# Dropless mixture of experts: when expert numbers, positions and one look-ahead element are read and made

## What is computed

```
h = layernorm(x)
logits = h @ rw.T + rb                    # 896 tokens, 8 experts
vals, idx = top_k(logits, 2); gates = softmax(vals)
h1 = gelu(h @ fc1_w[e] + b1[e]); eo = h1 @ fc2_w[e] + b2[e]
x = x + sum over the two chosen experts of gates * eo
...
k = ctx @ kw + kb; v = ctx @ vw           # second cross attention: of ctx alone
out = softmax(q k / 4) v
```

## Time and profile before

| | |
|---|---|
| median of 3 runs | 2123.18 us (2117.42 to 2124.7) |
| profiled execution, its own time | 2124.0 us |
| its span | 2122.2 us |
| granted TensorE clock, mean share | 0.923 |
| busy: PE, DVE, ACT, POOL | 84%, 62%, 41%, 29% of the span |
| the mixture | from 366 to 653 us of the span |
| its tile loop | from 449.65 to 620.4 us |
| loads of each tile | 1028 KB and 1024 KB of weights (first, second layer), 128 KB of rows; 128 KB of results stored |
| DMA share in the tile loop | 0.83 (464 to 541 us), 0.89 (541 to 613 us) |

### The profile page before, as it was taken

How to read it: one execution, slowest core, us unless ns; L and a number is a source line. 1 busy time by engine, 2 the same in 40 slices (tenths; PEclk the granted TensorE clock), 3 DMA queues, 4 the chain that set the end, 5 groups by cost and what they waited for, 6 DMA issues and landing times.

```text
span 2122.2 us, 34231 instructions
## 1 busy us (share of the span) xinstructions
PE 1787.3 (84%) x10658; PEld 1245.8 (59%) x10658; DVE 1323.6 (62%) x3343; ACT 860.9 (41%) x2497; POOL 618.0 (29%) x710
## 2 busy tenths in 40 slices
PE   5959997769995878998889999696886979999888
PEld 4736664558974756555755554483443845555557
DVE  5856776101115877788667767596776866656655
ACT  3735553223223642555334444242331434544421
POOL 2325554200011233676500000040000325555433
PEclk9979999789997988899889999797998989999979
DMA  4000000368972001112100010101001000000200
GB/s 165 32 23 16 15 8 27 116 223 303 305 234 105 0 1 38 45 49 83 65 15 15 8 67 0 50 1 60 0 0 43 28 1 11 22 10 11 70 1 18
DMA packets 38632, 121.21 MB, mean 57 GB/s; under 512 B 2960, under 2 KB 26032, under 8 KB 31360
## 3 DMA queue, kind: packets, MB, share of 16 engines
q1 hardware_dynamic: 32520, 104.71, 14.5%
q10 hardware_dynamic: 4472, 11.52, 1.5%
q0 software_dynamic: 1536, 3.67, 0.6%
HBM read 102.41 MB, written 17.47 MB: 56 GB/s over the span
## 4 chain that ended last, share of the span: by engine, by line
PE 46%; issue 20%; POOL 13%; DVE 11%; ACT 4%; DMA 2%; another core or an unknown queue 1%; ACTq 1%; POOLq 0%; SPq 0%; DVEq 0%
POOL arena L1902 11%; PE ps L954 8%; PE ps L989 4%; PE ps L774 3%; PE ps L826 3%; PE ps L878 3%; PE ps L1114 3%; PE ps L896 3%; PE ps L1098 3%; PE ps L769 3%; PE ps L844 2%; PE ps L816 1%; PE ps L1033 1%; DMA arena<-rows_hbm 1%
## 5 line engine op out<-in xcount | busy, mean ns | idle before, releaser
L1902 POOL TENSOR_TENSOR arena<-arena,rinv 112x375 f32<-112x375 f32 (+1 forms) x448 | 371.2, 830 | 505.9 <-DVE rinv L1570 494.2
L844 PEld LDWEIGHTS ps<-cst,arena 112*125 112x125 f32 (+1 forms) x1408 | 187.5, 183 | 176.1 <-POOL arena L1902 91.7
L844 PE MATMUL ps<-cst,arena 112*125 112x112 f32 (+1 forms) x1408 | 245.8, 293 | 44.7 <-POOL arena L1902 44.0
L1227 ACT ACTIVATE arena<-ps,negmax 112x375 f32<-112x375 f32 (+1 forms) x384 | 190.8, 502 | 178.3 <-DVE negmax L1565 177.9
L1579 DVE COPY arena<-ps 125x336 f32<-125x336 f32 x384 | 191.1, 498 | 49.5 <-PE ps L844 47.3
L1950 POOL TENSOR_TENSOR w_split_sb<-wml,w_split_sb 128x512 fp32r<-128x512 f32 (+1 forms) x40 | 46.0, 1150 | 563.3 <-ACT w_split_sb L1276 561.4
L1565 DVE TENSOR_REDUCE negmax<-ps 112x1 f32<-112x375 f32 (+1 forms) x288 | 158.2, 549 | 79.2 <-PE ps L816 69.4
L954 PE MATMUL ps<-h_split_sb,w_split_sb 128*128 128x448 f32 x768 | 178.4, 382 | 8.3 <-DVE h_split_sb L1699 4.3
L1227 ACT ACTIVATE arena<-arena,negmax 112x112 f32<-112x112 f32 (+1 forms) x256 | 125.4, 491 | 134.4 <-DVE negmax L1554 94.5
L954 PEld LDWEIGHTS ps<-h_split_sb,w_split_sb 128*128 128x128 f32 x768 | 151.8, 199 | 24.0 <-issue 5.9
L769 PE MATMUL ps<-wat,arena 128*125 128x256 f32 (+1 forms) x608 | 151.3, 386 | 7.9 <-ACT arena L1174 7.3
(11 more groups left out here) (213 smaller groups left out, 3159.8 us busy)
## 6 DMA issues: line engine op xcount, KB each, us to landing
wml<-in_wm_L_moe SPq DMA_DIRECT2D x21, 1028.0 KB, 5.6
wml<-in_wm_L_moe SPq DMA_DIRECT2D x21, 1024.0 KB, 6.1
craw<-in_ctx SPq DMA_DIRECT2D x34, 375.0 KB
wml<-in_wm_L_m SPq DMA_DIRECT2D x3, 3072.0 KB, 13.9
values_hbm<-vz ACTq DMA_DIRECT2D x8, 750.0 KB
vz<-values_hbm SPq DMA_DIRECT2D x8, 750.0 KB
wat<-in_wa_L_ca SPq DMA_DIRECT2D x2, 2560.0 KB
wml<-in_wm_L_m SPq DMA_DIRECT2D x2, 2048.0 KB, 13.0
```

The costliest lines, as they stand in the source:

```text
L844: last = nc.tensor.transpose(ps[0:blk.kp, T_BANK + s % blk.t_banks, o:o + S], buf[:, i * blk.nk + q * blk.kp:i * blk.nk + (q + 1) * blk.kp ...
L1227: last = go(probs[0:S, s % blk.nprobs, i * nk:(i + 1) * nk], src[:, i * nk:(i + 1) * nk], ACT.Exp, scale=-1.0 if blk.mask == "input" else ...
L1902: pool.tensor_tensor(p3, p3, r3, ALU.mult).then_inc(scaled, 1)
```

## The change

SyncE reads an expert number right before the load that needs it (the loads of tile t + 2 stand behind the wait for the gelu of tile t). The first rows are loaded ahead of the first second-layer weights. VectorE counts, for each token position, the experts chosen over the batches, so two matmuls are enough; it makes the part within a position itself (`within`) and adds it to the slots. Look-ahead element 4 is made behind `tile_results(18)`. The look-ahead stores values without padding (375 KB), in a part of `vz` that the self attention doesn't use; the wait for the stores goes from the mixture's end to the first keys of that attention (ScalarE) and to GpSimd's work for the next MLP, where GpSimd zeroes that part again. In the cross attention the values are loaded to `craw`, and ScalarE spreads them into `vz` with three instructions per batch, at step 12 of the batch before.

```diff
@@ load_tiles
+                chosen = []
                 def load_w1(t):
                     o = WH * (t % 2)
+                    chosen.append(sp.value_load(expert[0:1, t:t + 1], min_val=0, max_val=E - 1))
...
-                chosen = [sp.value_load(expert[0:1, t:t + 1], min_val=0, max_val=E - 1) for t in range(NT)]
                 for t in range(2):
                     load_w1(t)
-                for t in range(2):
-                    load_w2(t)
                 sp.wait_ge(scattered, 16 * TOP * B)
                 for t in range(2):
                     load_rows(t)
+                for t in range(2):
+                    load_w2(t)
@@ load_context
                             sp.wait_ge(av_done, st["group"] + (m - 1) * 4)
+                            sp.wait_ge(values_spread, m - 1)
                         sp.dma_start(kT[:, m % 2], ...)
-                        sp.dma_start(vz[0:KP, m % 2], values_hbm[m])...
+                        sp.dma_start(craw[:, m % 2], values_hbm[m]...)...
@@ tensor, weigh
+                        if blk.ahead:
+                            pe.wait_ge(values_spread, count(0, 1, b, 1))
@@ tensor, mixture
-                mm(ps[0:S, 2, 0:B * E], upper, chosen, ...)
-                for b in range(B - 1):
...
-                       start=False, stop=b == B - 2, skip_group_check=True)
-                for b in range(B):
-                    last = mm(ps[0:S, 1, 0:E], all_ones, flags[:, b], start=b == 0, stop=b == B - 1)
-                last.then_inc(placed, 1)
-                for m in range(1, 5):
+                mm(ps[0:S, 2, 0:E], cs("upper", S, S), counts, start=True, stop=True)
+                mm(ps[0:S, 1, 0:E], cs("ones", S, S), counts, start=True, stop=True).then_inc(placed, 1)
+                for m in range(1, 4):
                     context_ahead(m)
...
                     tile_results(t)
+                    if t == NT - 3:
+                        pe.wait_ge(tile_act, 2 * (NT - 2))
+                        pe.wait_ge(tile_kept, NT)
+                        context_ahead(4)
+                        pe.wait_ge(ahead_done, 5 * NAHEAD)
@@ scalar, attention: piece
                     elif name in ("K0", "K1"):
+                        if n > 0 and not blk.cross and isinstance(m, int) and m == 0:
+                            for i in range(2):
+                                act.wait_ge(ahead_stored[i], 32 * (B // 2))
@@ scalar, attention
+                def spread_values(m):
+                    par = parity(m)
+                    act.wait_ge(kv_loaded[par], pair(m) * 32 + 32)
+                    if not isinstance(m, int) or m >= 2:
+                        act.wait_ge(av_done, count(st["group"], 4, m, -4))
+                    for q in range(KC):
+                        dst = vz[0:kp, par, q * H * 32:(q + 1) * H * 32]
...
+                        last = go(dst, craw[:, par, q]..., ACT.Copy)
+                    last.then_inc(values_spread, 1)
                 for name in blk.pieces:
                     piece(0, name)
+                if blk.ahead:
+                    act.wait_ge(zeroed, 3)
+                    spread_values(0)
                 def body(b):
                     for s in steps(b, blk, lag + 1):
+                        if blk.ahead and s == 12 and more(b):
+                            spread_values(b + 1)
@@ scalar, context_ahead
-                        for i, q in enumerate([0, 1] if c == 0 else [2]):
-                            dst = vz[0:KP, m % 2, q * H * 32:(q + 1) * H * 32]
...
+                        last = go(v_ahead[:, m % 2, 0:2 * D] if c == 0 else v_ahead[:, m % 2, 2 * D:3 * D], W[0:KP, 0:(2 - c) * D], ACT.Copy)
@@ scalar, mixture
-                for m in range(5):
+                for m in range(4):
                     context_ahead(m)
...
+                    if t == NT - 2:
+                        context_ahead(4)
                 for m in range(5, B):
                     context_ahead(m)
-                for i in range(2):
-                    act.wait_ge(ahead_stored[i], 32 * (B // 2))
@@ vector, mixture
-                v.tensor_scalar(flags, rank, float(TOP), None, ALU.is_lt).then_inc(flagged, 1)
+                link(v.tensor_scalar(flags, rank, float(TOP), None, ALU.is_lt))
+                by_expert = flags.rearrange("p b e -> p e b")
+                v.tensor_reduce(counts, by_expert, AX_X, ALU.add).then_inc(flagged, 1)
+                for b in range(B):
+                    last = v.tensor_tensor(big1[:, b], by_expert, early[:, b]..., ALU.mult)
+                link(last)
+                link(v.tensor_reduce(within, big1, AX_X, ALU.add))
...
+                link(v.tensor_tensor(slots, slots, within, ALU.add))
@@ gpsimd, feed_forward
+                if n + 1 == AHEAD_AT:
+                    for i in range(2):
+                        pool.wait_ge(ahead_stored[i], 32 * (B // 2))
+                    pool.memset(vz[:, :, H * 32:KC * H * 32], 0.0).then_inc(zeroed, 1)
```

More of the change, by code:

```diff
@@ L350, in build @@
         over = in_arena(E * (B * S // P), S).rearrange("p (e j) -> p e j", e=E)
-        ntiles, tile0, until = (in_arena(E, S) for _ in range(3))
+        ntiles, tile0, until, counts = (in_arena(E, S) for _ in range(4))
+        within = in_arena(B * E, S).rearrange("p (b e) -> p b e", b=B)
+        assert B == E
         before = in_arena(E * E, S).rearrange("p (i j) -> p i j", i=E)
@@ L439, in build @@
         ahead_stored = [sem("ahead_stored0"), sem("ahead_stored1")]
+        values_spread = sem("values_spread")
         kv_loaded = [sem("kv_loaded0"), sem("kv_loaded1")]
@@ L1064, in mixture @@
                 pe.wait_ge(flagged, 1)
-                upper, all_ones = cs("upper", S, S), cs("ones", S, S)
-                chosen = flags.rearrange("p b e -> p (b e)")
-                mm(ps[0:S, 2, 0:B * E], upper, chosen, start=True, stop=False, skip_group_check=True)
-                for b in range(B - 1):
-                    later = flags[:, b].unsqueeze(1).broadcast_to([S, B - 1 - b, E])
-                    mm(ps[0:S, 2, (b + 1) * E:B * E].rearrange("p (b e) -> p b e", e=E), all_ones, later,
-                       start=False, stop=b == B - 2, skip_group_check=True)
-                for b in range(B):
-                    last = mm(ps[0:S, 1, 0:E], all_ones, flags[:, b], start=b == 0, stop=b == B - 1)
-                last.then_inc(placed, 1)
-                for m in range(1, 5):
+                mm(ps[0:S, 2, 0:E], cs("upper", S, S), counts, start=True, stop=True)
+                mm(ps[0:S, 1, 0:E], cs("ones", S, S), counts, start=True, stop=True).then_inc(placed, 1)
+                for m in range(1, 4):
                     context_ahead(m)
@@ L1239, in evacuate @@
                     last.then_inc(o_done, 1)
+                def spread_values(m):
[5 more added lines that the diff above has]
+                        dst = vz[0:kp, par, q * H * 32:(q + 1) * H * 32]
+                        dst = bass.AP(tensor=dst.tensor, offset=dst.offset, ap=[list(dst.ap[0]), [64, 8], [48, 2], [1, 16]])
+                        last = go(dst, craw[:, par, q].rearrange("p (a z d) -> p a z d", z=2, d=16), ACT.Copy)
+                    last.then_inc(values_spread, 1)
                 for name in blk.pieces:
                     piece(0, name)
+                if blk.ahead:
+                    act.wait_ge(zeroed, 3)
+                    spread_values(0)
                 def body(b):
                     for s in steps(b, blk, lag + 1):
+                        if blk.ahead and s == 12 and more(b):
+                            spread_values(b + 1)
                         if b != B:
@@ L1777, in mixture @@
                 link(v.tensor_reduce(rank, big1, AX_X, ALU.add))
-                v.tensor_scalar(flags, rank, float(TOP), None, ALU.is_lt).then_inc(flagged, 1)
+                link(v.tensor_scalar(flags, rank, float(TOP), None, ALU.is_lt))
+                by_expert = flags.rearrange("p b e -> p e b")
+                v.tensor_reduce(counts, by_expert, AX_X, ALU.add).then_inc(flagged, 1)
+                for b in range(B):
+                    last = v.tensor_tensor(big1[:, b], by_expert, early[:, b].unsqueeze(1).broadcast_to([S, E, B]), ALU.mult)
+                link(last)
+                link(v.tensor_reduce(within, big1, AX_X, ALU.add))
                 dve.wait_ge(gate_exp, 2)
```

13 lines of the change are left out of this document (6 added, 7 removed).

## The result

The changed kernel takes 2100.39 us (median of 6 runs, 2093.44 to 2106.68) against 2122.55 us of the kernel before (median of 6, 2117.42 to 2131.8). The ratio is 0.9877, 95% interval 0.9853 to 0.99. Three later comparisons on other occasions gave 0.9897, 0.9894 and 0.9894, so the gain is 22 to 26 us; I had forecast 15. The profiled execution spans 2099.7 us where the one before spanned 2122.2.

A forecast was written before the change was run, and what follows sets the result against it. Bounds: 21 reads delaying weights, rows and ScalarE before the tiles; TensorE nearly full in the loop. Tiles -7.3, mixture's end -8.3, cross attention -1.8 and +1: -16.4 from 2124.0, so 2108; range 2097 to 2121, its own case 2103 to 2117 (0.6).

The forecast's parts named there:

- The start of the tiles: Ahead of the mixture's tiles: the first tile starts at 427.4 instead of 449.65, 22.2 us gained.
- 4 of 34 records: Position matmuls ahead of the scatter: two matmuls leave 4 of 34 records, taking 2.8 us less on TensorE.
- A warmer first tile: First tile of the mixture: a gap under 3 us leaves TensorE's clock higher, 2.3 us gained.
- Element 4: Tile loop: look-ahead element 4 moves in from before the tiles, uncovered on TensorE, 8.2 us added.
- The reads in the loop: Tile loop: 19 expert-number reads ahead of the loads; half of each lands on a tile, 9 us added.
- cheap reads: Rival, tile loop: reads cost 200 ns, or landing shortens by what they add; 2101 us, chance 0.18.
- The mixture's end: Mixture to next self attention: ScalarE's first copy no longer waits for the last store, 8.3 us gained, at worst 6.5.
- The MLP ahead of the cross attention, GpSimd's zeroing: GpSimd zeroes 2048 values a partition in 1.8 us, covered by its 12.85 us wait for TensorE: 0.
- The cross attention's start: First scores: smaller loads stop deciding, 1.8 us gained, 2.1 at best, 0 at worst.
- The cross attention's loop: Three ScalarE copies for each further batch, 1.1 us, mostly covered: 1 us added, from 0 to 8.
- ScalarE's blocked queue: Rival, ahead of the tiles: element 3's stores hold ScalarE, first tile 12.5 us later; 2120 us, chance 0.12.
- Dear reads: Rival, tile loop: a full read at the highest price lands on every tile, 34 us instead of 9; 2133, chance 0.08.

The follow-up runs named there:

- e4: The kernel before, with 16 added 128x128 matmuls on TensorE in the idle ahead of the cross attention's first scores: 2125.8 us, ratio 0.998.
- e1: The changed kernel with all 21 expert numbers read before the first weights, as before: 2117.37 us, ratio 0.994.
- e5: The changed kernel with two extra spreads on GpSimd, so TensorE idles longer ahead of the cross attention's first scores: 2106.51 us, ratio 0.9884.
- the second e2: The changed kernel with each read moved ahead of SyncE's wait for the gelu, repeated with more runs: 2100.54 us, ratio 0.9877.
- e9: The changed kernel with added matmuls filling TensorE's idle at every boundary from an MLP to an attention: 2095.38 us, ratio 0.9846.

## Why the forecast was right in kind and short in size

- **The start of the tiles** (forecast -22.2): right. 449.65 - 426.32 = 23.3 us, or 24.3 counted from the flags, and it was there in every trace of the changed kernel. Undone one at a time, the parts are worth 12.7 us (reads), 3.3 (order of the loads) and 9.3 (element 4, which the loop takes back). With the compact values alone the first tile came 6 us earlier too; how much of that is theirs is open. ScalarE's issues didn't stay under 1 us ahead of the first tile, as I had said they would (7.56 and 2.62), and that cost little. My "4 of 34 records" was a slip: L1067, L1070 and L1073 have 32; nothing was computed from it.
- **A warmer first tile** (forecast -2.3): wrong. 6.48 us against 6.07. I had reasoned that a short gap leaves the clock up. It was up from 418 on, and at half again from 425, behind a stretch from 421.8 to 426.3 in which TensorE had 1.2 us of work (the gates' and the rows' transposes). With four reads, with element 4 first and with the weights first, it was full there, and the interval from the first to the second tile was 4.97 us instead of 7.6.
- **Element 4** (forecast +8.2): right; the interval is 15.38 - 7.25 = 8.1 us longer (8.4 to 10.5 in the other three traces).
- **The reads in the loop** (forecast +9): the step that failed. I took 1.0 us a read from rows that stood beside the scatter, where they were the only ones. In the loop a read has 0.267 + 0.152 us, some 0.55 with its gaps. In the experiment with four, 0.22 us of each added read landed, near half of it as in my rule; for 19 reads that is 4.2 us. The differences between the kernels with and without reads in the loop say 1 to 2. The stage didn't look as I had drawn it either. I had 8.05 us per early tile growing to 8.5 and TensorE waiting for rows at most tiles; of the first 12 intervals after, six are still 8.05 us, as many as before, and TensorE waited for rows at 8 of the tiles. So the loop is not without slack at every tile, and how much of a single read lands stays open between nothing and half. I gave the cheap reads a chance of 0.18 and let the median of the earlier trace rows speak against them, although it was taken under another load. The Trainium skill ("Runtime: NRT & Kernel Launch", section "Instruction fetch mechanics") has about 200 ns for a register load. For the load itself the trace is near to it in the loop (267 ns) and far from it beside the scatter (672).
- **The mixture's end** (forecast -8.3): right. From the last tile's results to the self attention's first scores 50.80 became 42.04 us, -8.8 (42.0 to 44.6 over the four traces).
- **The MLP ahead of the cross attention, GpSimd's zeroing** (forecast 0): right. Its hidden-layer matmuls took 37.0 us before, 37.1 to 38.2 in the four traces after, and 37.1 with the compact values alone. The self attention ahead of it, from first scores to the MLP's start, took 117.7 us before and 119.7 to 121.1 in the four traces after. In e4, which leaves this stage as it was, it took 119.2, and in three variants of the changed kernel (e1, e5, the second e2) 118.1, so part of this is spread; it was not followed up.
- **The cross attention's start** (forecast -1.8): right, 19.33 - 17.48 = 1.85, with GpSimd's spread as the new last wait.
- **The cross attention's loop** (forecast +1): the second miss. The copies cost 0.1 us a batch, 0.5 to 0.7 in all. But I looked at the clock at the start of the tiles only, and not here, where the same profile showed 1.60 us for four scores up to 857 and 0.89 from 861 on. With the shorter idle ahead of it the stage, copies included, was 3.1 us shorter in the first trace, and 0.4 to 3.1 over the four.

The sum with what the runs showed: -23.3 + 0 + 8.1 + 4.2 - 8.8 - 1.85 - 1.8 (the middle of the last item) = -23.5, where 22 to 26 were measured and I had -16.4. That it comes out so well is partly luck. It takes the reads at the slope of the added ones and leaves out what the two traces show elsewhere: 3.5 us more in the self attention and the MLP, 1.9 less behind the cross attention, and a loop that grew by 4.7 instead of 4.2. Of the 7 us between, 5 are the reads, 3 the cross attention's loop, 1 the start, and the first tile's clock goes 2 the other way. The rival of cheap reads had 2101, which is the measured time to within 1 us. Its premise, a read far cheaper than my 1.0 us, is what the loop shows; but its number also needs the luck that the cross attention's 3 us and the first tile's 2 us, which it had not, nearly cancel. ScalarE's blocked queue, the rival at 2120, came in a milder form: 2.62 us ahead of the first tile, not 13. Dear reads, the rival on the other side, would need a price like that of four reads per tile, which gave 2121.69 us, no gain left.

## What to carry to other kernels

Take the price of an operation from rows that stand under the load it will meet, not under the one it leaves: the same read took 0.27 us in the tile loop and 0.42 to 0.71 beside a scatter (medians of four traces). When work is moved onto a full engine from ahead of a stage, expect its time back there in full. And when a wait of a few microseconds goes, look at what the clock does behind it: here that was worth 0.4 to 3.1 us beside a wait that shrank by 1.85. Where a stage varies by several microseconds from one trace to the next, as this loop did, take a small price from an edit that repeats the cost several times, and say that it is the price of the added ones.

## What the hardware showed beyond expectation

- The clock behind an idle of TensorE. With 2.75 us of idle ahead of the first scores it was back 3.5 or 7.8 us behind them; with 4.54 or 4.63 us, 15 us behind them; with the 4.6 us filled by matmuls of no use, 2 us ahead of them. Kept up across the boundary in e9, it fell 5 us behind the first scores, where in the changed kernel it fell 10 us ahead of them, and was back another 10 us later. Ahead of this fall TensorE had been busy for 5.57 us of the 8 from 820 to 828; the fall came at 833.7, when it was full again.
- A store from ScalarE's queue can stand in the issue: 7.56 us for 375 KB beside the scatter and 2.1 MB of weights, 9.85 for 750 KB beside 4.1 MB of weights, 2.62 for 375 KB beside 2.1 MB, 0.34 elsewhere. What holds it was not tried. ScalarE does nothing in that time. TensorE stood 5.54 us beside the first of these, which the profile puts down to issue.
- The wait for the last store at the mixture's end hardly hangs on its size: 8.87 us for 750 KB and 8.30 for 375. What it hangs on was not tried.
- SyncE's reads beside the scatter take 29 us for 21 in three of the four kernels that have them there (395.6 to 425.0, 393.7 to 423.4 and 393.3 to 422.6) and 23.5 in the fourth (394.8 to 418.3), and single ones 1.4 us.
